# Opening passes by channel half, two orders on VectorE: a feed-forward layer on one Trainium2 core

## The reference, cut to what matters

```python
x_filtered = ifft(fft(x_quat, axis=1) * spectral_gate, axis=1).real   # one gate per lane: a scale
x_rotated = hamilton(q_left_n, hamilton(x_filtered, q_right_conj))    # a 4x4 rotation per lane
probs = softmax(xf @ Wr.T)                                            # 8 experts, the last is used
h = gelu(xf @ W1[7] + b1[7], approximate=False)
out = x + (h @ W2[7] + b2[7]) * probs[:, 7:8]
```

## Time and profile before

| | us |
|---|---|
| median of 3 runs | 102.83 (102.68 to 104.61) |
| the profiled execution | 102.29 |
| its span, first to last instruction | 100.5 |
| mean granted TensorE clock (share of full speed) | 1.000 |
| PE busy | 96.4 (96%) |
| PEld busy | 80.7 (80%) |
| DVE busy | 67.3 (67%) |
| ACT busy | 58.1 (58%) |
| POOL busy | 25.7 (26%) |

### The profile page before, as it was taken

One profiled execution on the slowest core, in us unless ns is written; L12 is line 12 of the kernel. 1 busy time (PEld: TensorE's weight loads), 2 busy tenths in 40 slices (PEclk: granted clock), 3 DMA queues, 4 the chain that ended last, 5 costly groups with the idle time before them and its releaser, 6 DMA issues.

```text
span 100.5 us, 1483 instructions
## 1 busy us (share of the span) xinstructions
PE 96.4 (96%) x516; PEld 80.7 (80%) x516; DVE 67.3 (67%) x137; ACT 58.1 (58%) x101; POOL 25.7 (26%) x20
## 2 busy tenths in 40 slices
PE   6899999999999999999999999999999999999980
PEld 7689888888878888878888888888888888888970
DVE  1579798789965699923241694699328697656560
ACT  0669999964969944923426945865509944443600
POOL 3314000000000000005999999994000000000000
DMA  3979999965984000000000100001441810350014
GB/s 64 312 180 261 278 204 208 193 134 133 213 187 176 0 0 0 7 0 0 0 0 1 2 7 2 2 0 30 101 79 11 175 25 0 82 124 9 0 45 164
DMA packets 20822, 8.57 MB, mean 85 GB/s; under 512 B 17872, under 2 KB 19408, under 8 KB 20816
## 3 DMA queue, kind: packets, MB, share of 16 engines
q1 hardware_dynamic: 20096, 7.69, 35.2%
q10 hardware_dynamic: 720, 0.79, 2.5%
HBM read 6.36 MB, written 2.10 MB: 84 GB/s over the span
## 4 chain that ended last, share of the span: by engine, by line
PE 92%; DMA 2%; DVE 2%; issue 0%; DVEq 0%
PE pre L910 41%; PE acc L933 22%; PE acc L937 11%; PE acc L947 5%; PE acc L955 4%; PE pre L865 3%; DMA quats<-in_small 2%; PE lT_bank L854 2%; PE acc L822 1%; PE acc L951 1%; PE acc L949 1%; PE acc L839 1%; DVE y L715 1%; PE lT_bank L839 0%; DVEq L77 0%
## 5 line engine op out<-in xcount | busy, mean ns | idle before, releaser
L460 ACT ACTIVATE h_hi<-pre,quats 128x512 fp32r<-128x512 f32 x32 | 22.0, 689 | 29.2 <-PE pre L910 28.2
L648 DVE TENSOR_TENSOR h_lo<-h_all,h_hi 128x512 fp32r<-128x512 f32 x32 | 22.0, 688 | 20.9 <-ACT h_all L462 20.6
L933 PE MATMUL acc<-h_hi,w_parts 128*128 128x512 f32 x96 | 25.7, 389 | 0.0
L910 PE MATMUL pre<-xT_lo,w_hi 128*128 128x512 f32 x60 | 23.5, 392 | 0.0
L910 PE MATMUL pre<-xT_hi,w_hi 128*128 128x512 f32 x60 | 23.5, 392 | 0.0
L388 POOL TENSOR_TENSOR exps<-e_const,shifted 128x32 f32<-128x32 f32 x4 | 22.0, 5533 | 0.1
L462 ACT ACTIVATE h_all<-pre,quats 128x512 f32<-128x512 f32 x32 | 21.8, 682 | 0.0
L933 PEld LDWEIGHTS acc<-h_hi,w_parts 128*128 128x128 f32 x96 | 18.0, 188 | 3.8
L910 PE MATMUL pre<-xT_hi,w_lo 128*128 128x512 f32 x60 | 18.5, 390 | 0.0
L937 PE MATMUL acc<-h_lo,w_parts 128*128 128x512 f32 x48 | 14.8, 389 | 0.0
L910 PEld LDWEIGHTS pre<-xT_lo,w_hi 128*128 128x128 f32 x60 | 11.3, 188 | 2.4 <-DVE xT_lo L566 0.3
(11 more groups left out here) (89 smaller groups left out, 89.7 us busy)
## 6 DMA issues: line engine op xcount, KB each, us to landing
x_sq<-in_x SPq DMA_DIRECT2D x12, 128.0 KB, 3.3
w<-in_W SPq DMA_DIRECT2D x4, 256.0 KB, 5.9
w_last<-in_W_last SPq DMA_DIRECT2D x4, 256.0 KB, 6.9
out<-out_sq SPq DMA_DIRECT2D x8, 128.0 KB, 2.9
x_sq<-in_x SPq DMA_DIRECT2D x8, 64.0 KB, 3.5
w_late<-in_W_late SPq DMA_DIRECT2D x4, 128.0 KB, 3.5
x_last<-in_x SPq DMA_DIRECT2D x1, 512.0 KB, 4.6
out<-out_sq SPq DMA_DIRECT2D x8, 64.0 KB, 2.2
```

The costliest lines, as they stand in the source:

```text
L460: nc.scalar.activation(h_hi[:, s, :], pre_bank(b, f)[:, :], ACT.Gelu, bias=b1_cols[:, f:f + 1]).then_inc(h_hi_ready, 1)
L648: nc.vector.tensor_tensor(h_lo[:, s, :], h_all[:, s, :], h_hi[:, s, :].bitcast(F32), ALU.subtract).then_inc(h_lo_ready, 1)
L910: last = nc.tensor.matmul(bank[:, :], w[:, k, cols], part_of_x[:, k, :], start=(n == 0), stop=(n == len(steps) - 1))
L933: nc.tensor.matmul(sums(b, k), w2_parts[:, f, i, k * P:(k + 1) * P], h_hi[:, s, :], start=(f == 0 and i == 0), stop=False)
```

## The change

Three edits in the order of instructions. No instruction is added or dropped.

1. In `opening()` the passes over one half go by channel group: `w1_hi` for tiles 0 and 1, then `w1_lo` for both, with k = 0, and then all again with k = 1. The waits go along: each group waits for its own part of x and W1. The `xT_lo` passes keep their order, each with its own wait.
2. In DVE's block 0 `sum_last_w1(1)` and `late_w1_low(4)` stand ahead of `low_hidden(0, 5)`, and `late_w1_low(5)` stands right behind it.
3. In DVE's start `rotation(0)` stands ahead of `terms_of(1)`.

```diff
@@ DVE, rotation
             sums_of(0)
-            terms_of(1)
             dve.wait_ge(lane_eye_ready, 1)
             rotation(0)
+            terms_of(1)
             dve.wait_ge(squares_ready, 2)
@@ DVE, block 0
                 if b == 0:
                     sum_last_w1(0)
+                    sum_last_w1(1)
+                    late_w1_low(4)
                     low_hidden(b, 5)
-                    late_w1_low(4)
-                    sum_last_w1(1)
+                    late_w1_low(5)
                     turn_x(1, 0)
-                    late_w1_low(5)
                     split_w2(3)
@@ PE, opening()
+                for half in range(2):
                     for k in range(KC):
-                        last = nc.tensor.matmul(...)
-                    return last
-
-                pe.wait_ge(w1_first_hi_ready, KC)
-                for half in range(2):
-                    pe.wait_ge(first_xT_hi_ready, KC * (half + 1))
-                    for f in range(2):
-                        products(w1_hi, xT_hi, half, f)
-                    if half == 0:
-                        pe.wait_ge(w1_first_lo_ready, KC)
-                    for f in range(2):
-                        products(w1_lo, xT_hi, half, f)
+                        if half == 0:
+                            pe.wait_ge(w1_first_hi_ready, k + 1)
+                        pe.wait_ge(first_xT_hi_ready, KC * half + k + 1)
+                        for f in range(2):
+                            product(w1_hi, xT_hi, half, f, k)
+                        if half == 0:
+                            pe.wait_ge(w1_first_lo_ready, k + 1)
+                        for f in range(2):
+                            product(w1_lo, xT_hi, half, f, k)
                     if half == 0:
                         fold(2)
                 for f in range(2):
                     for half in range(2):
-                        pe.wait_ge(first_xT_lo_ready, KC * (half + 1))
-                        last = products(w1_hi, xT_lo, half, f, ends=(half == 1))
+                        for k in range(KC):
+                            pe.wait_ge(first_xT_lo_ready, KC * half + k + 1)
+                            last = product(w1_hi, xT_lo, half, f, k, stop=(half == 1 and k == KC - 1))
```

More of the change, by code:

```diff
@@ L859, in opening, with product @@
             def opening():
-                def products(w, part_of_x, half, f, ends=False):
+                def product(w, part_of_x, half, f, k, stop=False):
                     tokens = slice(half * HALF, (half + 1) * HALF)
+                    return nc.tensor.matmul(pre_bank(0, f)[:, tokens], w[:, k, f * P:(f + 1) * P], part_of_x[0][:, k, tokens],
+                                            start=(w is w1_hi and part_of_x is xT_hi and half == 0 and k == 0),
+                                            stop=stop, skip_group_check=True)
+                for half in range(2):
                     for k in range(KC):
-                        last = nc.tensor.matmul(pre_bank(0, f)[:, tokens], w[:, k, f * P:(f + 1) * P], part_of_x[0][:, k, tokens],
-                                                start=(w is w1_hi and part_of_x is xT_hi and half == 0 and k == 0),
-                                                stop=(ends and k == KC - 1), skip_group_check=True)
-                    return last
-                pe.wait_ge(w1_first_hi_ready, KC)
-                for half in range(2):
-                    pe.wait_ge(first_xT_hi_ready, KC * (half + 1))
-                    for f in range(2):
-                        products(w1_hi, xT_hi, half, f)
-                    if half == 0:
-                        pe.wait_ge(w1_first_lo_ready, KC)
-                    for f in range(2):
-                        products(w1_lo, xT_hi, half, f)
+                        if half == 0:
[7 more added lines that the diff above has]
+                            product(w1_lo, xT_hi, half, f, k)
                     if half == 0:
```

## The result

The changed kernel takes 102.26 us (median of 11 runs, 101.83 to 102.70), the kernel before 102.68 (11 runs, 102.36 to 104.61). The ratio is 0.9954, with a 95% interval of 0.9935 to 0.9974: 0.47 us faster, between 0.27 and 0.67. That is within 2%. The run of 104.61 is a slow one (2% above the kernel's fastest) and isn't in the ratio. The forecast was -0.42 and 102.4; the 102.4 counts from a median before of 102.83 in three runs, which eleven runs put at 102.68.

What follows compares the result with a forecast made beforehand. PE was taken to bound the kernel, with 92% of the chain of waits. PE's 0.41 us opening gain would meet DVE's 0.42 limit, so 102.83 - 0.42 = 102.41, forecast 102.4, range 101.8 to 103.0.

Steps and rivals of the forecast that it cites:

- The opening's two waits: Ahead of each opening half PE waits for the later `xT_hi`, losing 0.29 and 0.31 us; splitting ends the opening 0.41 earlier.
- first opening pass near 6.45: Sign in PE's timeline: the first opening pass starts near 6.45 to 6.5 us and not at 6.65.
- The stall at block 1's first product: PE loses 0.14 us in block 1's first product, whose load waits for block 1's second `xT_lo`.
- None of this moves with the opening: DVE's first six sums, from 19.30, follow ACT's start at 18.79, which waits for DMA `w_last`, so they stay put.
- up to 28 us the two edits don't add: PE, 0.41 us earlier from the opening, waits 0.13 for block 1's second `xT_lo`; the total is DVE's 0.42.
- PE's load there still waits, 0.1 to 0.3: Sign at block 1's second `xT_lo`: PE's load still waits for DVE, 0.1 to 0.3 us.
- minimum of two limits: If the opening gives g, the total gain is the smaller of 0.42 us and g + 0.14.
- Tile 6's `w_lo` just in time: DVE's later `w_lo` of tile 6 allows PE's pass at 23.01, wanted at 23.10: in time by 0.09 us.
- Edit 3 at nothing: In DVE's start, `rotation(0)` first gains 0 (bounds 0 to 0.08); other work comes 0.13 later, dying in DMA waits.
- C: Rival, slower: waits on nearly every opening pass stop weight loads running ahead, 0.08 each; +0.11 us, 102.94; chance 0.08.
- D: Rival: TensorE's clock falls over the opening's 24 passes, 2.8 us more, 105.6; chance 0.02.

Runs made afterwards that it cites:

- opening_only: The kernel before with only the opening's passes reordered by channel group, with their waits: 102.34 us, 0.49 us faster than before (0.25 to 0.74).
- no_rotation_edit: The changed kernel without moving `rotation(0)` ahead of `terms_of(1)`: 0.65 us faster than the kernel before (0.39 to 0.90), ratio 0.9937.
- seven_warm_ups: The changed kernel without the `rotation(0)` move and with seven warm-up matmuls in place of six: 0.56 us faster than the kernel before (0.34 to 0.77).
- order_without_early_waits: The changed kernel with the old waits for both channel groups at the head of each opening half: 0.17 us faster than the kernel before (-0.03 to 0.37).
- rotation_only: The kernel before with only `rotation(0)` moved ahead of `terms_of(1)`: 0.02 us faster than before (-0.15 to 0.21), ratio 0.9998.
- changed_again: The changed kernel itself, run and traced once more: 0.55 us faster than the kernel before (0.32 to 0.77), ratio 0.9947.

## Why the prediction was right

The time, the range and the sign held, but the formula that joined the two edits was wrong, and that it gave nearly the measured number was luck. Point by point:

- **The opening's two waits, and 0.41 us for edit 1: right, in size too.** With TensorE at full rate by the first half, the opening ends 3.29 to 3.31 us after DVE's start on x, in four kernels with edit 1, and 3.72 to 3.74 in four without early waits: 0.42. opening_only measures 0.49. In the forecast's own terms, the second half's hi passes end 2.30 to 2.31 after that start in opening_only, no_rotation_edit and seven_warm_ups, where 2.29 was forecast and before has 2.76; the lo passes then take 0.99 to 1.00 in place of 0.96, so 0.03 of the gain goes where 0.06 was forecast. The mark "first opening pass near 6.45" was met, by the records' starts, where the rate was up (6.21, 6.41 and 6.49 in the same three) and not in the changed kernel's own traces (7.20, 7.55).
- **The stall at block 1's first product, 0.14 us: right.** It is 1.50 to 1.52 in the four kernels without edit 2 and 1.36 with it. Edit 2 is worth 0.16.
- **"None of this moves with the opening", and so "up to 28 us the two edits don't add": wrong.** In the trace of before two limits stand side by side. ACT ended the sums, which had waited for the DMA `w_last`, at 18.79 + 1.28 = 20.07; PE ended tile 5's product at 19.43 + 0.61 = 20.04; and gelu of tile 5, from which DVE's wait for `h_all` follows, began at 20.08:

```profile
19.43 0.61 PE L910 MATMUL pre<-xT_hi,w_lo 128*128 128x512 f32 x2
...
20.08 0.69 ACT L460 ACTIVATE h_hi<-pre,quats 128x512 fp32r<-128x512 f32 x1
```

  In that one execution a faster PE would indeed have met the DMA. But it is the only one of the thirteen traces in which ACT waits for `w_last`; in the other twelve the sums are done before, and gelu of tile 5 waits 0.17 to 0.29 us for PE. I had taken one late landing for a fixed limit. opening_only's 0.49 shows that edit 1's 0.42 passes through. With edit 2's 0.16 that makes 0.58 with the array at full rate (0.65 measured without edit 3; 0.56 with seven warm-ups). How often `w_last` comes late enough to bind, no run here tells.
- **"PE's load there still waits, 0.1 to 0.3": wrong, by the same step.** With edit 2 no trace has a wait for block 1's `xT_lo`.
- **The total, 0.42 forecast, 0.47 and 0.55 measured.** The forecast's minimum of two limits was the wrong formula with nearly the right value. It also left out executions in which TensorE is late through its rate and edit 1 has less wait to remove. That these make the measured total smaller than 0.58 is argued from two traces (differences 3.82 and 4.13); the intervals don't separate 0.5 from 0.58, so there may be nothing to explain.
- **Tile 6's `w_lo` just in time: it didn't bind.** In the changed kernel's trace it ends at 22.79 + 0.41 = 23.20 and its pass starts at 23.87. The sums begin when PE lets them, so an earlier PE doesn't eat up this distance: in no_rotation_edit they are 22.69 and 23.36.
- **Edit 3 at nothing: not contradicted.** Alone it measures 0.02 faster (-0.15 to 0.21), the later second `R` and `scale` included; a cost of some 0.1 us would not show.
- **Rivals.** C (each wait costs the load's head start) fell: the eight lo passes with a wait each keep 0.12. D fell: alternating banks change neither the distance nor the rate, in order_without_early_waits and all others. The Trainium skill (TensorE: Matmul & The Clock Gate, "A second HAM failure mode: psum-queue depth-cycling") tells of clock swings in a kernel that cycles through banks with idle between; in the opening this kernel's banks change at passes that stand 0.12 apart, and no run here shows a swing.

## What to carry to other kernels

Where two releasers coincide within 0.03 us in the one trace at hand, the trace can't tell which of them an edit will meet. Work the sum out with each of them, and look in a second execution whether the one that is a DMA's landing still binds; here it did in one trace of thirteen. A wait for "all parts" ahead of a series of passes is worth splitting when the producer delivers the parts one by one and the consumer stands ready; the gain is the passes that fit ahead of the last part, 4 x 0.118 us here. A single trace can be 0.4 us off the typical one through TensorE's rate and a landing, so at this size compare differences between events, not end times.

## What the runs showed of the hardware

- The moment at which TensorE's rate doubles varies between executions of nearly the same program. With six or seven warm-ups the first full-rate distance came by about 4 us in three traces, within the first fold or at its end in others, at about 6.3 us in the changed kernel's first trace and in rotation_only, and at about 6.8 in changed_again; L822 x4 takes 1.21 to 2.26 us accordingly. In changed_again even the transposes run at half rate:

```profile
3.87 2.26 PE L822 MATMUL acc<-w_first,R 128*128 128x264 f32 x4 [0.20 <-DMA w_first<-in_W_first]
5.93 0.63 PE L832 MATMUL acc<-ident,x_first 128*128 128x128 f32 x2
6.35 0.64 PE L832 MATMUL pre<-ident,x_first 128*128 128x128 f32 x2
6.78 1.12 PE L839 MATMUL acc<-w_second,R 128*128 128x256 f32 x4
```

  The granted clock reads 0.995 to 1.000 over each of these spans, and 1.00 in the stretch of the half-rate fold itself (3.9 to 5.9 us of changed_again). The Trainium skill (TensorE: Matmul & The Clock Gate, "What you observe") lets this point vary by about 0.5 us from run to run; the spread here is some 3 us (3.9 to 6.8).
- With four warm-ups fewer, ended 1.7 us earlier, the rate rose only at about 9.3 to 9.5 us, and the kernel before took 1.1 us more.
- The last landing of the same four 64 KB DMAs, issued at nearly the same times, lets DVE begin between 6.61 and 7.08 us in the seven traces where it waits for them and SP issues all four. The rest of the program keeps its length, so that moves its end one for one.
